# One decoder layer on one core: its five hand-written lists of steps in another order

## The reference

```python
x = x + attn(layernorm(x))            # part A: q, k, v = x@w (head size 128); softmax(q k^T / sqrt(128)) v, masked, times w_o
x = x + xattn(layernorm(x), ctx)      # part B: xp = relu(x W^T + b), yp = relu(ctx W^T + b)
                                      #         softmax(xp yp^T, masked keys left out) @ ctx
x = x + ffn(layernorm(x))             # part C: rows of x rounded to 8 bits; silu(x gate) * (x up), hidden 1024;
                                      #         rows rounded to 8 bits again; times down. The weights are made ternary
```

## Time and profile before

| | |
|---|---|
| median of 3 runs | 356.8 us (355.89 to 358.05) |
| the profiled execution | 354.63 us |
| its span, first to last instruction | 352.8 us |
| TensorE, weight loads | 333.2 us (94%), 219.3 us (62%) |
| VectorE, ScalarE, GpSimd | 299.5 us (85%), 284.7 us (81%), 295.7 us (84%) |
| mean granted TensorE clock | 0.995 of full speed |
| DMA queue of SP | 54.04 MB, its packets took 72.1% of 16 engines' span |

### The profile page before, as it was taken

How to read it: one execution, slowest core, us unless ns; L and a number is a source line. 1 busy time by engine, 2 the same in 40 slices (tenths; PEclk the granted TensorE clock), 3 DMA queues, 4 the chain that set the end, 5 groups by cost and what they waited for, 6 DMA issues and landing times. The chain is left out here.

```text
span 352.8 us, 6993 instructions
## 1 busy us (share of the span) xinstructions
PE 333.2 (94%) x1812; PEld 219.3 (62%) x1838; DVE 299.5 (85%) x862; ACT 284.7 (81%) x532; POOL 295.7 (84%) x503
## 2 busy tenths in 40 slices
...
GB/s 278 409 110 224 109 182 173 104 166 113 103 131 179 106 162 247 153 123 145 153 212 209 98 198 181 148 90 207 218 130 68 102 175 164 33 126 134 71 121 120
DMA packets 132264, 54.49 MB, mean 154 GB/s; under 512 B 124672, under 2 KB 126336, under 8 KB 131840
## 3 DMA queue, kind: packets, MB, share of 16 engines
q1 hardware_dynamic: 132224, 54.04, 72.1%
...
## 5 line engine op out<-in xcount | busy, mean ns | idle before, releaser
L711 POOL TENSOR_TENSOR b_p<-b_p 128x512 f16<-128x512 f32 x32 | 37.2, 1165 | 5.7 <-ACT b_p L1001 5.6
L1092 ACT ACTIVATE c_work<-g_bank,c_tanh_scale 128x512 f32<-128x512 f32 x52 | 35.4, 680 | 7.6 <-PE g_bank L1418 5.4
L1685 DVE TENSOR_TENSOR c_work<-c_work,u_bank 128x512 f32<-128x512 f32 x52 | 35.3, 679 | 2.4 <-PE u_bank L1418 1.3
L1205 PE MATMUL b_bank<-c,b_p16T 128*128 128x256 f16 x128 | 34.9, 273 | 1.6 <-DMA b_p16T<-b_p 1.4
L1690 DVE SCALAR_TENSOR_TENSOR c_work<-c_work,g_bank 128x512 f32<-128x512 f32 x50 | 33.9, 677 | 2.2 <-ACT c_work L1092 1.9
L707 POOL TENSOR_TENSOR p<-a_p,p 128x512 f16<-128x512 f32 x28 | 32.3, 1165 | 3.7 <-ACT p L946 3.6
L1661 DVE CUSTOM_DVE_ANT_0 b_p<-b_bank,mask_add,s_scale 128x512 f32<-128x512 f32 x32 | 23.7, 742 | 13.8 <-PE b_bank L1207 8.5
L1206 PE MATMUL b_bank<-c,b_p16T 128*128 128x256 f16 x128 | 34.9, 273 | 0.0
L1207 PE MATMUL b_bank<-c,b_p16T 128*128 128x256 f16 x128 | 34.9, 273 | 0.0
L1418 PE MATMUL u_bank<-upT,xqT 128*128 128x512 bf16 x104 | 31.7, 380 | 1.7 <-DVE c_work L1685 1.3
L1438 PE MATMUL d_bank<-downT,c_half 128*128 128x256 bf16 x240 | 31.2, 273 | 1.2 <-DMA c_half<-c_half 0.8
...
## 6 DMA issues: line engine op xcount, KB each, us to landing
...
c_work<-in_w_up SPq DMA_DIRECT2D x1, 1024.0 KB, 9.5
c_work<-in_w_gate SPq DMA_DIRECT2D x1, 1024.0 KB, 7.3
c_half<-in_w_down SPq DMA_DIRECT2D x1, 1024.0 KB, 8.9
```

What stands on the lines that cost most here:

```text
L711: pool.tensor_tensor(b_p16[:, t, S:2 * S], b_p[:, t, :], b_p16[:, t, 0:S], ALU.subtract).then_inc(b_p_los, 1)
L1092: act.activation(gate_tile(j, n), gu_bank("g", j, n), ACT.Silu if (n, j) in SILU else ACT.Tanh, scale=c_tanh_scale[:, j // 2:j // 2 + 1]). ...
L1205: pe.matmul(dst, l_hi, r_hi, start=first, stop=False)
L1685: dve.tensor_tensor(h_tile(j // 2, n)[:, (j % 2) * HALF:(j % 2 + 1) * HALF], gate_tile(j, n), gu_bank("u", j, n), ALU.mult).then_inc(hs, 1)
```

## The change

The five lists are written in another order. They hold the same steps, each once; no operation, tile, bank or transfer is added or taken away, and neither is a line of the code that a step runs. The order was found by a search that made transfers late at random. One list line less makes every line number of the code below the lists smaller by one. Of the diff a few lines of each list stand for the rest:

```diff
 PE_ORDER = """
-    W.sumQ/0 W.sumK/0 W.sumV/0 A.Q/0 A.K/0 A.V/0 W.r/0 A.S0/0 A.S1/0 W.ws/0 A.VT/0 A.S2/0 W.vs/0 E.SS/1 E.YP0/0
...
-    A.S2/1 A.Y1/0 A.S3/1 A.Q/2 A.K/2 F.total/0 B.XT0/0 B.XT1/0 E.SS/2 B.XP0/0 B.XP1/0 A.H/1 B.S0/0 B.S1/0 A.Y0/1
...
-    B.XT1/1 B.XP0/1 B.XP1/1 A.H/2 B.S0/1 C.g0/0 A.Y0/2 B.S1/1 C.g1/0 C.u0/0 A.Y1/2 B.S2/1 C.u1/0 A.Q/3 E.SS/3 B.S3/1
...
-    B.XT1/5 C.u7/3 A.S0/6 C.DN1/3 B.XP0/5 B.XP1/5 A.S1/6 C.g0/4 A.S2/6 A.S3/6 C.DN2/3 C.u0/4 B.S0/5 C.DN3/3 C.g1/4
...
-    B.O2/7 C.u4/6 C.u5/6 B.O3/7 C.g6/6 C.xT0/7 C.u6/6 C.g7/6 C.DN3/5 C.g0/7 C.u7/6 C.g1/7 C.u0/7 C.DN0/6 C.u1/7
...
+    W.sumQ/0 W.sumK/0 W.sumV/0 A.Q/0 A.K/0 A.V/0 W.r/0 A.S0/0 W.ws/0 A.S1/0 A.VT/0 A.S2/0 E.SS/1 E.YP0/0 A.S3/0
+    A.P0/0 A.P1/0 E.YP1/0 W.vs/0 A.Q/1 A.P2/0 A.K/1 A.P3/0 A.V/1 A.H/0 E.SS/0 E.YP0/1 A.S0/1 A.S1/1 A.Y0/0 F.total/0
+    E.YP1/1 A.S2/1 A.Y1/0 A.S3/1 A.Q/2 A.K/2 E.SS/2 B.XT0/0 B.XT1/0 B.XP0/0 B.XP1/0 A.H/1 B.S0/0 A.Y0/1 B.S1/0
...
+    E.YP1/2 B.XP0/1 B.XP1/1 A.H/2 C.g0/0 B.S0/1 C.u0/0 A.Y0/2 B.S1/1 C.g1/0 C.u1/0 E.SS/3 B.S2/1 B.S3/1 A.Y1/2
...
+    C.g7/3 A.V/6 C.u7/3 B.XP0/5 B.XP1/5 A.S0/6 C.DN1/3 C.g0/4 C.u0/4 A.S1/6 A.S2/6 B.S0/5 A.S3/6 B.S1/5 C.DN2/3
+    B.S2/5 C.g1/4 C.DN3/3 E.YP0/6 C.u1/4 C.g2/4 B.S3/5 C.u2/4 E.YP1/6 C.g3/4 C.u3/4 A.H/6 C.g4/4 C.u4/4 B.O0/5
...
+    C.g4/6 C.g5/6 C.u4/6 B.O2/7 C.u5/6 C.u6/6 C.g6/6 C.g7/6 C.DN2/5 C.u7/6 B.O3/7 C.xT0/7 C.DN3/5 C.g0/7 C.xT1/7
...
 ACT_ORDER = """
-    E.hi/0 A.exp0/1 A.exp1/1 E.YP1/1 A.P1/1 A.P0/1 A.exp2/1 B.norm0/0 A.exp3/1 A.P2/1 A.P3/1 A.K/2 B.norm1/0 E.sq/2
...
-    A.exp1/2 A.P1/2 A.exp2/2 A.P2/2 A.exp3/2 A.P3/2 B.XT0/1 B.XT1/1 C.norm0/0 F.sign3/0 B.XP0/1 B.XP1/1 F.sign4/0
...
+    E.hi/0 A.exp0/1 A.P0/1 E.YP1/1 A.exp1/1 A.P1/1 B.norm0/0 A.exp2/1 A.exp3/1 A.P2/1 A.P3/1 A.K/2 E.sq/2 B.norm1/0
...
+    A.exp2/2 A.P2/2 A.exp3/2 B.norm1/1 A.P3/2 E.YP0/2 B.XT0/1 B.XT1/1 C.norm0/0 B.mask/1 F.sign4/0 B.XP0/1 B.XP1/1
...
 SP_ORDER = """
-    W.qkv/0 W.t1/0 W.t0/0 W.x0/0 W.x1/0 W.W/0 S.xT/1 W.o/0 S.x/1 S.ctx/1 W.c/0 F.up/0 S.xT/2 F.gate/0 S.rw/1 S.cT0/1
-    S.rb/1 S.mask/0 S.ctx/0 S.cT1/1 F.down/0 S.ctx/2 S.vT/1 S.pT0/1 S.mask/1 S.pT1/1 S.pT2/1 S.pT3/1 S.xT/3 S.cT0/2
+    W.qkv/0 W.t0/0 W.t1/0 W.x1/0 W.x0/0 W.o/0 S.x/1 W.W/0 S.xT/1 S.ctx/1 W.c/0 F.up/0 F.down/0 F.gate/0 S.xT/2
+    S.rw/1 S.cT0/1 S.ctx/0 S.cT1/1 S.mask/0 S.rb/1 S.vT/1 S.ctx/2 S.pT0/1 S.mask/1 S.pT1/1 S.pT2/1 S.pT3/1 S.cT0/2
```

More of the change, by code:

```diff
@@ L118 @@
[L118 to L127, removed]
@@ new lines @@
+    C.g2/0 C.u2/0 A.Q/3 A.K/3 C.g3/0 B.O0/1 A.V/3 C.u3/0 C.g4/0 B.O1/1 A.S0/3 C.g5/0 B.O2/1 B.O3/1 A.S1/3 B.XT0/2
+    B.XT1/2 C.u4/0 C.g6/0 A.S2/3 E.YP0/3 C.u5/0 B.XP0/2 B.XP1/2 A.S3/3 C.u6/0 C.DN0/0 C.g7/0 C.u7/0 E.YP1/3 B.S0/2
+    C.g0/1 B.S1/2 C.u0/1 C.DN1/0 B.S2/2 C.g1/1 B.S3/2 C.u1/1 C.DN2/0 C.g2/1 A.H/3 C.DN3/0 C.u2/1 A.Y0/3 A.Y1/3
+    C.g3/1 E.SS/4 C.u3/1 B.O0/2 B.O1/2 A.Q/4 C.g4/1 B.O2/2 A.K/4 C.u4/1 B.O3/2 C.g5/1 B.XT0/3 C.u5/1 B.XT1/3 A.V/4
+    C.g6/1 A.S0/4 B.XP0/3 B.XP1/3 C.u6/1 C.g7/1 C.DN0/1 C.u7/1 A.S1/4 A.S2/4 E.YP0/4 A.S3/4 B.S0/3 B.S1/3 C.g0/2
@@ new lines @@
+    B.S2/3 C.u0/2 C.g1/2 E.YP1/4 B.S3/3 C.DN1/1 C.u1/2 C.g2/2 C.DN2/1 C.u2/2 A.H/4 E.SS/5 C.g3/2 C.DN3/1 A.Y0/4
+    A.Y1/4 C.g4/2 C.u3/2 B.O0/3 A.Q/5 C.g5/2 C.u4/2 B.O1/3 C.u5/2 A.K/5 C.g6/2 B.O2/3 B.O3/3 B.XT0/4 A.V/5 B.XT1/4
+    C.g7/2 E.YP0/5 C.u6/2 B.XP0/4 B.XP1/4 C.DN0/2 C.u7/2 A.S0/5 E.YP1/5 C.DN1/2 C.g0/3 B.S0/4 A.S1/5 C.g1/3 C.u0/3
+    A.S2/5 C.DN2/2 B.S1/4 A.S3/5 C.g2/3 C.u1/3 C.DN3/2 B.S2/4 C.g3/3 C.u2/3 B.S3/4 C.u3/3 C.g4/3 B.O0/4 E.SS/6
+    C.u4/3 C.g5/3 A.H/5 C.u5/3 B.O1/4 A.Y0/5 A.Y1/5 C.g6/3 A.Q/6 C.DN0/3 B.O2/4 C.u6/3 B.O3/4 A.K/6 B.XT0/5 B.XT1/5
```

223 lines of the change are left out of this document (112 added, 111 removed).

## The result

| | before | changed kernel |
|---|---|---|
| median of 4 runs each | 357.12 us (355.89 to 358.05) | 350.01 us (349.63 to 351.09) |
| ratio, 95% interval | | 0.986 (0.9821 to 0.9898) |
| the profiled execution, its span | 354.63 us, 352.8 us | 351.09 us, 349.3 us |
| both measured again (medians of 20 and 6 runs) | 355.02 us | 350.78 us, ratio 0.985 (0.9811 to 0.9889) |

The change makes the kernel 1.4% faster, about 5 us by the ratio (3.6 to 6.4). The ratio is not the quotient of the two medians of four runs, which lie 7.1 us apart. All runs together, 70 of before and 10 of the changed kernel, have medians of 355.4 and 350.5 us, 4.9 apart. The two profiled executions differ by only 3.5 us. I had forecast −2.2.

What follows compares the result with a forecast made beforehand. TensorE, busy for 94% of the span, was taken to bound the kernel, with other engines close behind from 100 us. Terms −0.4 + 0 − 1.0 − 0.8 = −2.2 us took the median from 356.8 to 354.6 us; 8-in-10 range 351.0 to 360.0.

Steps and rivals of the forecast that it cites:

- The sign of being wrong that I had named: The prediction called itself wrong if the stretch 88 to 320 us moved by more than 2 us either way.
- 88 to 320 us: Middle: three transfer waits count −1.3 us, up and gate products close behind their pairs +0.3; sum −1.0, bounds −1.7 to +1.7.
- Start to 56 us: Start: ScalarE's idle time goes (−1.65 us), a later norm step (+1.06) and uncovered GpSimd work (+0.2) come; sum −0.4.
- it carries the gain on: Start: ScalarE, with the same steps and nearly no gap, keeps the 1.65 us won at the context step until `B.XT0/0`.
- The +1.06: Start: `B.norm1/0` now stands behind `E.sq/2` on ScalarE and TensorE cannot transpose before it, costing 1.06 us.
- 56 to 88 us: Waits of `B.XP0/1` and `B.S0/1` not shortened on balance, as ScalarE steps offset the fill: 0, bounds −2.0 to +1.3 us.
- The counted covers: Middle: TensorE work between feeding and needing steps; waits of `C.DN3/3` (0.35 us) and `B.O0/2` (0.82) go, `A.H/7`'s by half.
- The +0.3: Middle: up and gate products following their last pair in under 2 us lack a quarter more, costing 0.3 us.
- The end: From 320 us: `B.O3/7` loses its 1.09 us wait for its transpose, counted as −0.8 us, bounds −1.1 to +1.1.
- Traded waits: Rival, whole kernel: each cover that grows takes its work from another, so no change, 356.8 us; chance 0.33.
- The crowded start: Rival, start: three 1 MB loads together delay the context, so ScalarE's step starts 4.7 us later; 359.7 us, chance 0.14.
- Most hidden waits go: Rival: a third of the small waits in 100 to 300 us and one XP wait go, −6 us, 350.8; chance 0.08.

Runs made afterwards that it cites:

- e8: Changed kernel with `B.norm1/0` again ahead of `E.sq/2` on ScalarE and `E.SS/2` behind `B.XT1/0` on TensorE, as in before: 350.54 us, ratio 0.9878.
- e2: Splice: the old lists for steps that start before 88 us, the new order for all the rest: 353.1 us, ratio 0.9919 to before.
- e6: Kernel before with `C.u0/3`, `C.DN3/3` and also `C.DN3/5` (ahead of `B.O3/7`) moved on TensorE: 356.42 us, ratio 1.0032.
- e9: Kernel before with seven extra 512 KB transfers, one behind each result store of sequences 0 to 6: 362.59 us, ratio 1.0206.
- e11: Changed kernel with `F.total/0` on TensorE behind `A.K/2` again, as before the change: 350.44 us, ratio 0.9878 to before.
- e1: Splice: the new lists for steps that start before 88 us, the old order for all the rest: 354.31 us, ratio 0.9973 to before.
- e4: The changed kernel measured again, nothing altered: 350.78 us, ratio 0.985 to before.
- e7: Changed kernel with `B.O1/4` moved behind `A.Y0/5` and `A.Y1/5` on TensorE: 352.22 us, ratio 0.9894 to before.
- e10: Changed kernel with seven extra 512 KB transfers, one behind each result store of sequences 0 to 6: 355.11 us, ratio 1.0002 to before.
- e12: Changed kernel with sequence 6's load of `x` behind transpose `S.bT1/4` on SyncE, its VectorE statistics behind `C.bn0/4`: 350.33 us, ratio 0.9871 to before.
- e5: Kernel before with `C.u0/3` behind `A.S1/5` and `C.DN3/3` behind `C.g1/4` on TensorE: 356.69 us, ratio 1.0036.

## Why the prediction was right in direction and wrong in size

Faster was right. The size was not: −2.2 us forecast against −5.0 by the ratio and −3.5 between the two profiles. By the ratio the 356.8 us ahead of the prediction become 351.8, which lies at the edge of the wide range (351.0 to 360.0) and outside the forecast's own (352.5 to 356.7); the median of the four runs, 350.0, lies below both. The range held only because it was made wide for the rivals. The sign of being wrong that I had named came: the stretch from 88 to 320 us moved by more than 2 us. The measured values below are the differences of the table, so 60 and 90 us stand for 56 and 88. Step by step:

- **Start to 56 us: −0.4, measured +1.0.** The idle 1.65 us of ScalarE for `ctx_raw` did go, and its step starts 1.29 us earlier than in the earlier trace rows:

```profile
29.99 1.04 ACT L1046 ACTIVATE c<-ctx_raw 128x1024 f16<-128x1024 f32 x1
```

  But "it carries the gain on" was wrong. ScalarE now does `W.wo/0` (0.5 us, in before ahead of this step) behind it, waits 0.27 us for TensorE ahead of `E.YP0/1` and a little at other steps, and reaches the copy of `A.K/2` at 43.48 us in place of 43.69: 0.2 us are left. The +1.06 was wrong as well (e8), so two errors nearly cancelled. What I hadn't priced was the clock. `B.XP0/0` starts at 48.91 us, 0.17 later than before, and the 24 matmuls from there to `B.S0/0` take 0.85 us more; together these are the +1.0. TensorE stands idle for 2.44 us, now that `F.total` is gone from there, and again for 1.91 us (the row at 48.91 shown above):

```profile
45.14 0.38 PE L1314 MATMUL e_bank<-c_ss,ones 128*128 128x1 f32 x2 [2.44 <-ACT c L1046]
```

  Behind it the granted clock is 0.50 (1.2 GHz) for all of 49 to 54 us, where before had a mean of 0.66 in the same stretch:

```profile
49.00:54.00 5.00, 5.00 (x13) 1.65 (x13) 0.00 (x0) 1.80 (x3) 4.47 (x3) 0.50 0.59 157
54.00:55.00 1.00, 1.00 (x5) 0.40 (x4) 0.00 (x0) 0.78 (x2) 0.27 (x1) 0.67 1.01 373
```

  A matmul of 512 columns starts every 0.43 us there and every 0.22 at full clock. That the longer idle time keeps the clock low isn't shown: e2, e6 and e9 have the old idle times (about 1.0 and 2.0 us) and the same 0.72, and e11 with `F.total` back has it too. What does differ is how often it happens: none of 64 runs with the new start (the changed kernel, e1, e4, e7, e8, e10 to e12) has a mean clock above 0.990, and 19 of 66 runs of before have.
- **56 to 88 us: 0, measured −1.3.** I let ScalarE's two activations ahead of the copies cancel the filled gap. They didn't: the wait of 1.47 us became two of 0.34 with the six matmuls of `E.YP1/2` between them.

```profile
77.92 0.39 PE L1204 MATMUL e_bank<-c16T,w 128*128 128x512 f16 x1 [0.34 <-ACT yp_hi L1014]
...
79.72 0.39 PE L1204 MATMUL b_bank<-b_T,w 128*128 128x512 f16 x1 [0.34 <-DVE b_T L1648]
```

- **88 to 320 us: −1.0, bounds ±1.7, measured −3.7.** This is the step that failed. The counted covers were right for `C.DN3/3` and `B.O0/2`, and `A.H/7` went too, 1.7 us where I counted 1.3. The +0.3 for up products behind their pairs had the wrong sign: the sum of what they lack grew, and their waits for VectorE went from 1.3 us to none. So what they lack isn't what they wait for. The bounds were taken from the named waits alone, and so left out what lies in distances under 0.3 us, 1.4 us of the win by e1 and e4. Against that stand the new wait of 1.5 us and one of 0.5, which I didn't see. No experiment takes this gain apart by single moves (e5 tried two and gained nothing), so which of the moved steps make it stays open.
- **The end: −0.8, measured 0.** `B.O3/7` starts at 324.52 us with no wait, as forecast. The time came back at once in the norm chain of the last sequence (e6 shows it with one moved step), here with

```profile
327.47 0.38 PE L1417 MATMUL g_bank<-gateT,xqT 128*128 128x512 bf16 x1 [0.49 <-ACT xqT L1068]
331.30 0.59 PE L1417 MATMUL u_bank<-upT,xqT 128*128 128x512 bf16 x2 [0.68 <-DVE c_work L1684]
...
336.78 0.60 PE L1417 MATMUL g_bank<-gateT,xqT 128*128 128x512 bf16 x2 [0.48 <-ACT xqT L1068]
```

- **The rivals.** Traded waits, my second likeliest, is refuted by the time and by e2. The crowded start is refuted by the rows: the three loads took 10.2, 12.0 and 13.8 us from their issues at 6.2, 6.9 and 7.6 us, so all had landed by 21.5 us and not by 32. Adding up what each had taken in before was the error. `r_rows` was issued late all the same, at 20.85 us where before had 15.75, but the context was issued at 23.26 in place of 24.85, and ScalarE's step for it started earlier.

```profile
c_work<-in_w_up SPq DMA_DIRECT2D x1, 1024.0 KB, 10.2
c_half<-in_w_down SPq DMA_DIRECT2D x1, 1024.0 KB, 12.0
c_work<-in_w_gate SPq DMA_DIRECT2D x1, 1024.0 KB, 13.8
```

  "Most hidden waits go", with 350.8 us and a chance of 0.08, is what happened: somewhat more than a third of the lost distance and one XP wait, less what the clock cost. I held VectorE's 47 of 50 us against it, but that did not keep the gain away: the changed kernel shows 47.9 of 50. The rule on matmul busy share and weight loads that the prediction cites (the Trainium skill, Perfetto Trace Analysis, Identifying the Most-Contended Engine) pointed to this room. The room used was 4 us of 350, and the share of weight loads rose from 62% to 63%.
